# A graph and attention layer on one core: loads of x in two parts, and the parameter rows spread after two groups

## The reference

```
xn = layernorm(x)
x  = x + gnn(xn, src, dst) + linear_attention(xn)
x  = x + experts(layernorm(x))            # 8 experts, routed by Sinkhorn

gnn: el = (xn @ W_src + b_src) . attn_l   # 8 heads of 64
     er = (xn @ W_dst + b_dst) . attn_r
     e  = leaky_relu(el[src] + er[dst])   # 100000 edges, sorted by dst
     a  = softmax of e over the edges of one dst
     out[dst] = sum of a * (xn @ W_val + b_val)[src]
```

## Time and profile before

| | |
|---|---|
| median of 3 runs | 3184.9 us (3174.07 to 3187.08) |
| profiled execution, its span | 3182.6 us |
| TensorE busy | 2569.4 us, 81% |
| VectorE busy | 1621.1 us, 51% |
| ScalarE busy | 993.6 us, 31% |
| GpSimd busy | 2209.5 us, 69% |
| mean granted TensorE clock | 0.907 |
| DMA | 341.23 MB, mean 107 GB/s |

### The profile page before, as it was taken

One profiled execution on the slowest core, in us unless ns is written; L12 is line 12 of the kernel. 1 busy time (PEld: TensorE's weight loads), 2 busy tenths in 40 slices (PEclk: granted clock), 3 DMA queues, 4 the chain that ended last, 5 costly groups with the idle time before them and its releaser, 6 DMA issues.

```text
span 3182.6 us, 47522 instructions
## 1 busy us (share of the span) xinstructions
PE 2569.4 (81%) x10463; PEld 1790.9 (56%) x10464; DVE 1621.1 (51%) x2963; ACT 993.6 (31%) x2564; POOL 2209.5 (69%) x1847
## 2 busy tenths in 40 slices
PE   6689999999999989951676777777888988934998
PEld 3366677776677744420454556665666766723443
DVE  6612222222222269985854555555666666767232
ACT  2312222222222210020454444554555655600111
POOL 6287778777778777877877877777777777600454
PEclk9889999999999989985699998898988999955999
DMA  4341121111111133420566667777777777630111
GB/s 144 122 105 33 31 37 29 29 29 29 30 31 29 23 105 119 117 64 3 157 174 173 176 181 183 185 186 182 194 193 187 196 193 195 175 111 0 45 52 38
DMA packets 276032, 341.23 MB, mean 107 GB/s; under 512 B 164855, under 2 KB 184030, under 8 KB 275850
## 3 DMA queue, kind: packets, MB, share of 16 engines
q0 software_dynamic: 218672, 227.51, 31.6%
q1 hardware_dynamic: 51709, 93.57, 9.1%
q10 hardware_dynamic: 5594, 19.52, 1.7%
HBM read 285.65 MB, written 55.25 MB: 107 GB/s over the span
## 4 chain that ended last, share of the span: by engine, by line
POOL 41%; PE 19%; issue 16%; DMA 13%; DVE 8%; DVEq 2%; POOLq 0%; ACT 0%; ACTq 0%
POOL R L552 31%; PE ps L640 17%; DMA R<-val_tab,src_i 11%; POOL R L594 8%; POOL er_starts L565 2%; DMA work<-in_x_dram 1%; DVEq L239 1%; DVE R L1463 1%; DVE work L1557 1%; DMA R<-in_L_gnn_b_dst_dram 1%; PE ps L934 1%; DVEq L1463 1%; PE ps L664 1%; DVE R L1444 0%; DVE R L1500 0%
## 5 line engine op out<-in xcount | busy, mean ns | idle before, releaser
L640 PE MATMUL ps<-R,work 125*125 (+3 forms) x5240 | 1650.6, 470 | 225.7 <-DVE R L1463 207.2
L640 PEld LDWEIGHTS ps<-R,work 125*125 125x125 f32 (+2 forms) x5240 | 987.6, 195 | 795.0 <-issue 655.7
L552 POOL DMA_INDIRECT R<-el_tab,src_i x800 | 984.6, 1231 | 341.1 <-issue 288.7
L594 POOL DMA_INDIRECT R<-val_tab,src_i x800 | 978.7, 1223 | 280.7 <-issue 180.8
L1463 DVE TENSOR_TENSOR R<-R,ps (+1 forms) x800 | 521.2, 693 | 131.4 <-DVE ps L1452 125.6
L1113 ACT ACTIVATE work<-work 125x125 f32<-125x125 f32 x900 | 277.8, 309 | 500.0 <-PE ps L640 472.1
L640 PE MATMUL ps<-work,R 128*128 128x250 f32 x1600 | 359.5, 383 | 21.8 <-DMA work<-R 21.8
L1110 ACT ACTIVATE work<-work,negdst 125x125 f32<-125x125 f32 x900 | 353.6, 393 | 59.2 <-issue 34.5
L640 PEld LDWEIGHTS ps<-work,R 128*128 128x128 f32 x1600 | 308.9, 194 | 59.1 <-issue 21.8
L1452 DVE COPY ps<-R (+1 forms) x401 | 69.9, 175 | 299.2 <-POOLq L600 227.1
L1295 DVE TENSOR_TENSOR R<-ps,R 125x512 f32<-125x512 f32 x50 | 34.6, 692 | 358.1 <-PE ps L640 358.1
(11 more groups left out here) (256 smaller groups left out, 2186.0 us busy)
## 6 DMA issues: line engine op xcount, KB each, us to landing
work<-in_x_dram SPq DMA_DIRECT2D x33, 500.0 KB
R<-el_tab,src_i POOLq DMA_INDIRECT x800
R<-val_tab,src_i POOLq DMA_INDIRECT x800, 5.9
val_tab<-R SPq DMA_DIRECT2D x50, 253.9 KB
work<-R SPq DMA_DIRECT2D x25, 500.0 KB
work<-xm_tab SPq DMA_DIRECT2D x50, 250.0 KB
out_dram<-R SPq DMA_DIRECT2D x50, 250.0 KB
xm_tab<-work ACTq DMA_DIRECT2D x17, 500.0 KB
```

What stands on the lines that cost most here:

```text
L552: eng.indirect_dma_start(out=ELP[:, g, c, :], out_offset=None, in_=el_tab[:, :], in_offset=bass.IndirectOffsetOnAxis(ap=src_i[:, t:t + 1], ...
L594: eng.indirect_dma_start(out=ring[:, slot, :], out_offset=None, in_=val_tab[:, :], in_offset=bass.IndirectOffsetOnAxis(ap=src_i[:, 2 * u + ...
L640: return pe.matmul(o, l, r, start=start, stop=stop)
```

## The change

Every load of x in stage 1 becomes two DMAs, one for partitions 0 to 111 and one for 112 to 124, on the same queue and with the same semaphore, which now counts 32 a use. The spreading of the parameter rows becomes a function and is called after `turn(1)` and before `logits(0)`.

```
+XS = 112
...
-                eng.dma_start(x_in[g % NXI][0:P, :, :], by_tile(x)[:, 2 * g:2 * g + 2, :]).then_inc(x_loaded[g % NXI], 16)
+                for lo, hi in ((0, XS), (XS, P)):
+                    eng.dma_start(x_in[g % NXI][lo:hi, :, :], by_tile(x)[lo:hi, 2 * g:2 * g + 2, :]).then_inc(x_loaded[g % NXI], 16)
...
-            pe.wait_ge(S["elr_params"], 96)
-            pe.wait_ge(S["row_ready"], 1)
-            for r in range(4):
-                last = mm(ps[:, 4 + r, :], ones[0:1, :], s_rows[:, r, :])
-            last.then_inc(S["rows_spread"], 1)
+            def spread_params():
+                pe.wait_ge(S["elr_params"], 96)
+                pe.wait_ge(S["row_ready"], 1)
+                for r in range(4):
+                    last = mm(ps[:, 4 + r, :], ones[0:1, :], s_rows[:, r, :])
+                last.then_inc(S["rows_spread"], 1)
...
                     turn(g, b)
+                    if isinstance(g, int) and g == 1:
+                        spread_params()
                     if not isinstance(g, int) or g >= 1:
                         logits(g - 1, (b - 1) % 2)
...
             def load_x(g, b):
-                act.dma_start(x_in[b][0:P, :, :], by_tile(x)[:, bass.ds(2 * g, 2), :]).then_inc(x_loaded[b], 16)
+                for lo, hi in ((0, XS), (XS, P)):
+                    act.dma_start(x_in[b][lo:hi, :, :], by_tile(x)[lo:hi, bass.ds(2 * g, 2), :]).then_inc(x_loaded[b], 16)
...
             def stats(g, b, u):
-                v.wait_ge(x_loaded[b % NXI], 16 * (u + 1))
+                v.wait_ge(x_loaded[b % NXI], 32 * (u + 1))
```

## The result

| | before | changed |
|---|---|---|
| median of 22 runs each | 3179.57 us (3164.08 to 3195.45) | 3166.88 us (3157.38 to 3175.83) |
| ratio to before, 95% interval | | 0.9958 [0.9947, 0.9969] |
| profiled execution, its span | 3182.6 us | 3167.7 us |
| first gather of `el` (L552, now L554) | 152.37 us | 137.75 us |

The change takes 12.7 us off the median; the forecast was 13.1 us. The forecast time was 3172, from a median of 3184.9 before; the 22 runs of before have 3179.57, which makes up 5.3 us of the difference to 3166.88. The gain is within the half per cent that counts as no change, and clear of its interval.

What follows compares the result with a forecast made beforehand. Stage 1 was taken as bound by its x loads; with them split, the last store of `el` would land at 138.4 instead of 151.5, a gain of 13.1 us, giving 3172 us, range 3160 to 3183.

Steps and rivals of the forecast that it cites:

- The bound: Stage 1: x loads run on about 5 engines, 4.1 us each against 3.11 us a group, so loads bound it.
- The load's new time: Stage 1's split x load: 1.9 us at 270 GB/s instead of 4.1 us, below TensorE's 3.11 us a group.
- The moved spreading: Start of stage 1: spreading after `turn(1)` from 27.5, taking 7.16 us; fold 1.2 us later than before.
- The search's start: VectorE in stage 1: `stats(4)` at 51.9, then nine groups at 3.22 us, so the search starts at 80.9.
- The slow group: TensorE after the search: idle over 7 us, then half clock, with 5.73 us instead of 3.11 to the next turn.
- The next limits: Stage 1 without waits for x: VectorE's cycle comes next, then the 7.1 us search, then TensorE.
- The translation: After stage 1: if the last store of `el` lands d us sooner, the rest of the kernel starts d sooner.
- Rival A: Stage 1: no slow group after the search (2.6 us) and full-clock spreading (3.6): gain 16 to 19 us, 3167; chance 0.25.
- B: Stage 1's x loads: disjoint halves serialize, a load keeps its 4.1 us and still bounds; 3185 us; chance 0.07.
- C: Start of stage 1: x shares every engine with the weights, parameter rows land at 41.7; 3186, 1 us slower; chance 0.03.
- D: After stage 1: it ends 13 us earlier, but later stages return 8 of it; 3180 us; chance 0.10.

Runs made afterwards that it cites:

- late search: The changed kernel with the first half of VectorE's search moved behind the last `norm`, ahead of the second half: 3157.76 us, 0.9958 of before.
- split alone: The changed kernel with the spreading back at its old place ahead of `turn(0)`, loads of x still in two DMAs: 3157.03 us, 0.9952 of before.
- rows first: Against the kernel with split loads and spreading ahead of `turn(0)`: parameter rows loaded before the two weights, with their own semaphore; 3147.9 us, 0.9912 of before.

## Why the prediction was right, step by step

| step | predicted | measured in the changed kernel |
|---|---|---|
| spreading starts | 27.5 | 26.88 |
| fold starts | 34.7 | 34.18 |
| search starts | 80.9 | 80.89 |
| `turn(12)`, `turn(13)` | 90.9, 96.6 | 90.56, 95.17 |
| `turn(24)` | 130.8 | 129.37 |
| last store landed | 138.4 | 136.86 |
| gain, first gather | 13.1 | 14.6 |
| gain, median | 13.1 | 12.7 |

- **The bound** was read rightly: loads on 5 of 16 engines. The boundaries at 115 and 113 partitions show that it is the divisor and no other effect of two DMAs. The step from "25 loads take 102 us" to "not in before some 130" was not worked out: beside GpSimd's look-ups x moves at 108 GB/s (60 to 80 us), 4.7 us a load and not 4.1, and the loads pause while the buffers are full (43 GB/s in all from 47 to 51 us).
- **The load's new time** was taken as 1.9 us from the row with 270 GB/s. With x alone, 188 GB/s at a share of 0.72 would be 261 GB/s at full share, 2.0 us. That was right, and the comparison "which side of 3.11 us" was the right one. The boundary at 95 adds that a load has to be under it beside the look-ups too: 3.4 us by the same reckoning were 4.3 and 3.7 in the trace, and 8.5 us of waits came back.
- **The moved spreading** came where it was expected. The 0.6 us that it was early come from the load of the tops (one row of `dstT`, 3.1 KB, with which VectorE works ahead of `stats(0)`): `stats(0)` ran at 17.55 (18.15). The same changed kernel profiled again was 0.6 us earlier still, so this is no more than the scatter between executions. What the prediction did not ask is what the split does with the old order. It does better, by 2.1 us in the trace; the row lands at 24.03 instead of 26.17.
- **The search's start** came out to 0.01 us by luck, as two errors cancel: `stats(4)` ran at 51.16 and not 51.9, and VectorE's nine groups from there took 29.73 us, 3.30 each and not 3.22.
- **The slow group** was mis-sized: 4.61 us between `turn(12)` and `turn(13)`, 1.1 us less than the 5.73 of the earlier trace rows. The turn took the forecast 1.93; the 8 matmuls of `logits` behind it took 2.37 us, between the 3.44 of the same place in the chain of before and the 1.79 of the later groups, so TensorE left the half clock (1.2 GHz) in the middle of them. The granted clock is 0.64 from 90 to 95 us and 1.00 from 95 on. This is 1.1 us of the 1.5 by which the store was too late in the sum.
- **The next limits** were named in the right order: VectorE's cycle, the search, then TensorE. The late search confirms that the search and its slow group cost about 8 us of the groups' time.
- **The translation** was assumed one to one. The profiled spans gave 14.9 us for a shift of 14.6, the medians 12.7 with an interval of 10 to 17. That the median came within 0.4 us of the forecast is in part luck: in stage 1 the gain was 1.5 us larger than forecast, and the interval of the medians holds that as well as 13.1.
- **Rival A** (cheap ends): the spreading kept its 7.19 us, and of the slow group's 2.6 only 1.1 to 1.2 came, so for the most part no. **B** (no spreading over engines): refuted by the share of 0.72. **C** (the rows come late) names a real mechanism: they are last of 5.1 MB and landed at 24.03 with the split alone, where I had reckoned 20 at 270 GB/s. In the changed kernel, whose trace has no wait for them and so no time of landing, it cost nothing, hidden by `turn(1)`; loading them first shows what it hid. **D** (given back later): the intervals leave no room for 8 us lost; they cannot exclude 3.

## What to carry to other kernels

When a stream of loads holds the DMA engines at a third of their share, look at the partition count of one load before the order of the work: here 125 partitions ran on five engines and 113 on one, and a cut at 112, a multiple of 16, removed it. A removed bound uncovers the next: here the fold's start, where 7.5 us sooner were worth 2.6 us before the split, and 6.5 us sooner were worth 7.2 after it, and the cure was to load four rows of 2 KB ahead of two weights of 1 MB. Where the total times of one kernel scatter by up to 1% (3164 to 3195 us for the kernel before), the start of the first instruction after the stage tells in one profile what 20 runs hardly can.

## What the hardware showed that I had not expected

- More engines, less each: 5 engines moved 125 GB/s at a share of 0.33, 23.7 GB/s for each busy engine; in the changed kernel 188 GB/s came at 0.72, 16.3 GB/s each, and 282 GB/s at 1.04 (weights and x, 15 to 18 us), 16.9 each. Three times the engines gave 2.3 times the rate. No run shows why.
- Two DMA issues can be much dearer than twice one. The timeline of the changed kernel:

```profile
26.99 1.05 ACTq L987 DMA_DIRECT2D work<-in_x_dram  x2
...
56.32 1.57 ACTq L987 DMA_DIRECT2D work<-in_x_dram  x2
...
102.69 0.83 ACTq L987 DMA_DIRECT2D work<-in_x_dram  x2
```

  From the first one's start to the second one's end, the nine pairs took 0.79 to 2.07 us, 0.83 in the median, where one took 0.28; a single one of them took 0.34 us in the median and 1.57 at most. The price that the prediction put at 2.5 us if uncovered would so have been more like 5 (nine times 0.55, what a pair takes above the 0.28). ScalarE's wait for TensorE hid it: it still waited 20.6 us in sum for the turns.
- The spreading took 7.16 to 7.19 us in every kernel whose start was read, at half-clock pace, wherever it stood: after 7 us of idling (split alone), after two turns (the change), or 0.7 us behind the tops (rows first), with a granted clock of 1.00 in the windows that hold it. Matmuls of one row could be slow at any clock; what follows speaks for the clock. The 16 transposes right behind it took 3.48 to 3.60 us (before, split alone, rows first), where 16 at full pace take 2.14 (twice 1.07). The clock's column cannot settle it: it reads 1.00 from 48 to 52 us in the changed kernel, where `logits(0)` took 3.49 us, the half-clock pace, and 0.52 from 47 to 51 us in the kernel before, where it took 3.46. The durations, not that column, gave the right term.
